# A recommendation tower on one core: GpSimd folds the gathered rows twice between its gathers

## The reference

```python
e = jnp.stack([tbl_0[ids[:, 0]], ..., tbl_31[ids[:, 31]]], axis=1)
z = jnp.sum(e, axis=-1)                                     # 32 sums
outer = jnp.einsum('bpd,pde,bpe->bp', e[:, II], kernels, e[:, JJ])   # 496 pairs
h = jnp.concatenate([z, outer, dense_ctx], axis=1)          # 544 values
h = jnp.maximum(h @ W_top1 + b_top1, 0.0)                   # 512
h = jnp.maximum(h @ W_top2 + b_top2, 0.0)                   # 256
y = h @ W_top3
```

## Time and profile before

| | before |
|---|---|
| median of 3 runs | 1091.63 us |
| profiled execution | 1090.3 us |
| its span | 1088.1 us |
| granted TensorE clock, mean | 0.914 |
| PE busy | 863.0 us, 79% |
| DVE busy | 636.6 us, 59% |
| ACT busy | 569.1 us, 52% |
| GpSimd (POOL) busy | 483.7 us, 44% |
| 512 gathers | 483.0 us, 943 ns each |
| DVE row sums, L371 | 64, 676 ns each |
| DVE products, L386 and L399 | 512, 1219 and 1218 ns each |

### The profile page before, as it was taken

How to read it: one execution, slowest core, us unless ns; L and a number is a source line. 1 busy time by engine, 2 the same in 40 slices (tenths; PEclk the granted TensorE clock), 3 DMA queues, 4 the chain that set the end, 5 groups by cost and what they waited for, 6 DMA issues and landing times.

```text
span 1088.1 us, 15106 instructions
## 1 busy us (share of the span) xinstructions
PE 863.0 (79%) x4112; PEld 294.6 (27%) x4112; DVE 636.6 (59%) x579; ACT 569.1 (52%) x4209; POOL 483.7 (44%) x518
## 2 busy tenths in 40 slices
PE   0312103989896999999879899998959899999998
PEld 0100001323232333332222233332312233333333
DVE  0110002977784766667766775676847656778960
ACT  0000000687775705686676526676747227687961
POOL 5777771003536554555545554455355545510000
PEclk9866555999997999999989999999979899999999
DMA  9211110000101110111101110011011101100000
GB/s 350 80 27 27 27 26 7 1 1 12 20 14 23 19 21 15 20 20 20 21 17 20 18 20 17 19 20 21 14 21 19 20 17 20 19 7 2 2 1 0
DMA packets 19803, 28.39 MB, mean 26 GB/s; under 512 B 8900, under 2 KB 9412, under 8 KB 18824
## 3 DMA queue, kind: packets, MB, share of 16 engines
q0 software_dynamic: 16384, 16.81, 8.4%
q1 hardware_dynamic: 3336, 10.63, 2.6%
HBM read 27.40 MB, written 0.01 MB: 25 GB/s over the span
## 4 chain that ended last, share of the span: by engine, by line
PE 63%; another core or an unknown queue 17%; issue 6%; DVE 6%; ACT 3%; DMA 2%; POOL 1%; SPq 1%; DVEq 0%; POOLq 0%
PE m_ps L498 27%; PE acc L526 14%; PE m_ps L513 9%; DVE prod L386 4%; PE tr L426 2%; ACT turned L323 2%; PE tr L446 2%; PE tr L456 2%; PE tr L450 2%; DMA w_sb<-in_w 2%; DVE turned L399 2%; POOL gathered L237 1%; PE tr L443 1%; PE m_ps L500 1%
## 5 line engine op out<-in xcount | busy, mean ns | idle before, releaser
L237 POOL DMA_INDIRECT gathered<-in_tbl,idx x512 | 483.0, 943 | 476.0 <-DVE prod L386 128.3
L386 DVE TENSOR_TENSOR prod<-m_ps,x_t 128x1024 f32<-128x1024 f32 x384 | 459.2, 1219 | 314.2 <-remote 169.5
L323 ACT ACTIVATE turned<-turned 128x64 f32<-128x64 f32 x2048 | 490.5, 241 | 105.1 <-DVE turned L399 86.5
L498 PE MATMUL m_ps<-x_t,k_sb 64*128 64x512 f32 x768 | 413.1, 641 | 138.2 <-DVE prod L386 67.7
L500 PE MATMUL m_ps<-x_t,k_sb 64*128 64x512 f32 x768 | 414.0, 642 | 0.0
L323 ACT ACTIVATION_READ_ACCUMULATOR turned<-turned 128x1 f32 x2048 | 384.5, 188 | 13.5 <-issue 13.3
L498 PEld LDWEIGHTS m_ps<-x_t,k_sb 64*128 64x128 f32 x768 | 130.8, 192 | 365.7 <-issue 272.2
L526 PE MATMUL acc<-prod,sel 128*32 128x512 f32 x1536 | 196.3, 631 | 0.0
L399 DVE TENSOR_TENSOR turned<-m_ps,gathered 128x1024 f32<-128x1024 f32 x128 | 155.9, 1218 | 60.1 <-PE m_ps L513 22.5
L274 ACT ACTIVATE x_t<-tr 128x512 f32<-128x512 f32 x64 | 37.6, 587 | 244.8 <-remote 155.0
L513 PE MATMUL m_ps<-k_sb,x_t 64*128 64x512 f32 x512 | 138.7, 618 | 6.7 <-DVE turned L399 6.7
(11 more groups left out here) (36 smaller groups left out, 113.4 us busy)
## 6 DMA issues: line engine op xcount, KB each, us to landing
gathered<-in_tbl,idx POOLq DMA_INDIRECT x512
k_sb<-in_kmat SPq DMA_DIRECT2D x7, 1024.0 KB, 11.3
w_sb<-in_w SPq DMA_DIRECT2D x1, 1280.0 KB
k_sb<-in_kmat SPq DMA_DIRECT2D x2, 256.0 KB, 3.3
k_sb<-in_kmat SPq DMA_DIRECT2D x1, 512.0 KB, 5.4
w_sb<-in_w SPq DMA_DIRECT2D x1, 512.0 KB
idx<-in_ids SPq DMA_DIRECT2D x1, 256.0 KB, 2.7
z_sb<-in_dense_t SPq DMA_DIRECT2D x4, 32.0 KB
```

The lines of the kernel that those rows point to most:

```text
L237: nc.gpsimd.indirect_dma_start(out=gathered[:, t, G % GR, f * D:(f + 1) * D], out_offset=None, in_=tables[2 * (STAGES - 1 - a) + f], in_of ...
L323: last = nc.scalar.activation(row, row, ACT.Copy, accum_out=z_turned[:, t, 16 * c + n:16 * c + n + 1])
L386: nc.vector.tensor_tensor(prod[:, r % PR, :, :], m_ps[:, p % MR, :, :], other, ALU.mult).then_inc(prod_ready, 1)
L498: nc.tensor.matmul(m_ps[:, p % MR, 0, :], k_sb[0:D, at, :], x_t[0:D, (q * STAGES + a0) % XR, :], start=True, stop=True)
```

## The change

Between its gathers GpSimd now also adds: when gather k - 4 has landed, `halve` adds the two halves of its 64 values into `x_half` (32 values, two places), and `fold` adds the two halves of that into `x_fold` (16 values, a ring of FR = 8 stages), one gather later. DVE's `sum_x` sums the 16 values of each row from `x_fold` and waits for the folds, not for the gathers. The ring of gathered stages is freed for the sums by the halving. Stages of later batches are transposed, copied and summed from step 97 on, 8.5 steps apart, and at the latest 4 steps in front of their first use, which for a = 0 to 15 is 97, 105, 114, 122, 131, 133, 136, 139, 146, 153, 163, 173, 186, 200, 216, 224; their gathers are asked for at the same steps as before. In batch 0, stages 14 and 15 stand at steps 86 and 90. The row sums are transposed at step 116, before at 80. `x_t` has room for 18 stages, before 20, and `y` is written into a row of `h2_sb`.

```diff
-XR = 20
+FR = 8
+XR = 18
...
-    return NS * (q - 1) + 82 + 8 * a
+    return NS * (q - 1) + min(97 + 17 * a // 2, NS + STEP_OF["even", FIRST[a]] - 4)
+
+
+def step_of_gather(q, a):
+
+    return NS * (q - 1) + 58 + 8 * a
...
-    AHEAD.setdefault((0, max(0, min(_s, 81 - 2 * (STAGES - 1 - _a))) if _a > 1 else 0), []).append(("x", 0, _a))
+    AHEAD.setdefault((0, max(0, min(_s, 90 - 4 * (STAGES - 1 - _a))) if _a > 1 else 0), []).append(("x", 0, _a))
...
-    AHEAD.setdefault((_q, 80), []).append(("s", _q, 0))
+    AHEAD.setdefault((_q, 116), []).append(("s", _q, 0))
...
+            def halve(k):
+                G, n = divmod(k, GATHERS)
+                t, f = divmod(n, 2)
+                at = gathered[:, t, G % GR, f * D:(f + 1) * D]
+                pool.wait_ge(gather_landed[k % IN_FLIGHT], (k // IN_FLIGHT + 1) * 16)
+                if k > 1:
+                    pool.wait_ge(x_folded, k - 1)
+                nc.gpsimd.tensor_tensor(x_half[:, k % 2, :], at[:, 0:D // 2], at[:, D // 2:D], ALU.add).then_inc(x_halved, 1)
+
+            def fold(k):
+                G, n = divmod(k, GATHERS)
+                t, f = divmod(n, 2)
+                pool.wait_ge(x_halved, k + 1)
+                if n == 0 and G >= FR:
+                    pool.wait_ge(x_summed, G - FR + 1)
+                nc.gpsimd.tensor_tensor(x_fold[:, G % FR, t, f, :], x_half[:, k % 2, 0:D // 4],
+                                        x_half[:, k % 2, D // 4:D // 2], ALU.add).then_inc(x_folded, 1)
...
+                if k >= IN_FLIGHT:
+                    halve(k - IN_FLIGHT)
+                if k > IN_FLIGHT:
+                    fold(k - IN_FLIGHT - 1)
+                if n == 0 and G >= GR:
+                    old_q, old_a = divmod(G - GR, STAGES)
+                    pool.wait_ge(tr_filled, place("x", old_q, old_a))
+                    pool.wait_ge(x_halved, (G - GR + 1) * GATHERS)
+                    if old_a // COLS:
+                        pool.wait_ge(prod_ready, old_q * NS + LAST_TURNED[old_a // COLS] + 1)
+                if q:
+                    pool.wait_ge(prod_ready, step_of_gather(q, a) + n)
+                col = ((q * STAGES + a) * 2 + f) * TILES + t
+                nc.gpsimd.indirect_dma_start(
...
 def keep_h2(q, n):
     act.wait_ge(tr_filled, place("h2", q, n))
+    if q and n == 0:
+        act.wait_ge(y_stored, 16 * q)
...
-                for landed in gather_landed:
-                    dve.wait_ge(landed, (G + 1) * GATHERS // IN_FLIGHT * 16)
+                dve.wait_ge(x_folded, (G + 1) * GATHERS)
...
-                                        gathered[:, :, G % GR, :].rearrange("p t (f d) -> p t f d", d=D),
+                                        x_fold[:, G % FR, :, :, :],
```

More of the change, by code:

```diff
@@ L160, in dlrm_tower @@
         z_sb = sb("z_sb", [P, NZ, QB])
+        x_half = sb("x_half", [P, 2, D // 2])
+        x_fold = sb("x_fold", [P, FR, TILES, 2, D // 4])
         z_nat = sb("z_nat", [P, 2, TILES, SUM_ROWS])
@@ L165, in dlrm_tower @@
         h2_sb = sb("h2_sb", [P, H2 // P, QB])
-        y_sb = sb("y_sb", [1, QB])
+        y_sb = h2_sb[0:1, 0, :]
         idx = sb("idx", [P, NQ * F * TILES], i32)
@@ L191, in dlrm_tower @@
         reduced = sem("reduced")
+        x_halved = sem("x_halved")
+        x_folded = sem("x_folded")
         x_summed = sem("x_summed")
@@ L217, in _ @@
             pool.wait_ge(idx_loaded, 16)
-            for G in range(NQ * STAGES):
-                q, a = divmod(G, STAGES)
[L220 to L240, removed]
@@ new lines, in _ @@
+            for k in range(NQ * STAGES * GATHERS):
+                G, n = divmod(k, GATHERS)
+                q, a = divmod(G, STAGES)
+                t, f = divmod(n, 2)
+                if k >= IN_FLIGHT:
[12 more added lines that the diff above has]
+                nc.gpsimd.indirect_dma_start(
+                    out=gathered[:, t, G % GR, f * D:(f + 1) * D], out_offset=None, in_=tables[2 * (STAGES - 1 - a) + f],
+                    in_offset=bass.IndirectOffsetOnAxis(ap=idx[:, col:col + 1], axis=0),
+                ).then_inc(gather_landed[k % IN_FLIGHT], 16)
@@ L242, in _ @@
+            for k in range(NQ * STAGES * GATHERS - IN_FLIGHT, NQ * STAGES * GATHERS):
+                halve(k)
+                fold(k - 1)
+            fold(NQ * STAGES * GATHERS - 1)
         @block.sync
@@ L260, in _ @@
                     sp.wait_ge(tr_kept, place("y", q - 1, 0))
-                    sp.dma_start(out[:, (q - 1) * QB:q * QB], y_sb[:]).then_inc(y_stored, 16)
+                    sp.dma_start(out[:, (q - 1) * QB:q * QB], y_sb).then_inc(y_stored, 16)
             sp.wait_ge(y_ready, 1)
-            sp.dma_start(out[:, LAST * QB:NQ * QB], y_sb[:]).then_inc(y_stored, 16)
+            sp.dma_start(out[:, LAST * QB:NQ * QB], y_sb).then_inc(y_stored, 16)
             sp.wait_ge(y_stored, 16 * NQ)
@@ L285, in keep_y @@
                 act.wait_ge(tr_filled, place("y", q, 0))
-                if q:
-                    act.wait_ge(y_stored, 16 * q)
-                nc.scalar.activation(y_sb[:], tr[0:1, :], ACT.Copy).then_inc(tr_kept, 1)
+                nc.scalar.activation(y_sb, tr[0:1, :], ACT.Copy).then_inc(tr_kept, 1)
             def keep_sums(q):
@@ L349, in _ @@
                                      bias=b1_sb[:, n:n + 1]).then_inc(h1_ready, 1)
+            act.wait_ge(y_stored, 16 * LAST)
             for n in range(H2 // P):
@@ L354, in _ @@
             act.wait_ge(y_summed, 1)
-            act.wait_ge(y_stored, 16 * LAST)
-            nc.scalar.activation(y_sb[:], tr[0:1, :], ACT.Copy).then_inc(y_ready, 1)
+            nc.scalar.activation(y_sb, tr[0:1, :], ACT.Copy).then_inc(y_ready, 1)
         @block.vector
```

## The result

The changed kernel takes 958.79 us (median of 4 runs, 958.0 to 959.47) where the kernel before took 1090.12 (4 runs, 1086.85 to 1092.18): a ratio of 0.8797, 95% interval 0.8771 to 0.8824. The forecast was 970, with a range of 930 to 1125. The profiled execution took 958.0 us, its span is 956.2. The size came out close; part of that closeness is errors that cancel, and the condition behind the gain turned out to be narrower than the prediction has it. "The standstill" is the state that the prediction describes: gathers go on, and the other engines hardly compute.

What follows compares the result with a forecast made beforehand. Gathers leaving GpSimd every 1.25 us were taken to bound the kernel by nearly stopping other engines. Spaced at 1.70, GpSimd's path gives 962 and PE's 946; 962 plus 8 for mutual waits gives 970 us, range 930 to 1125.

Steps and rivals of the forecast that it cites:

- The cause: Gathers back to back at 1.25 us nearly stop other engines; 130 us at the start and 39 a batch open.
- The period: GpSimd's gather spacing with both adds: 1.25 + 0.45 = 1.70 us, each add 0.13 plus about 0.1 issue.
- My term for GpSimd: GpSimd's whole path: 3.7 + 512 x 1.70 + 3 = 877, then landing, last steps, tail and outside: 962 us.
- PE's chain: Batch 0's first layer at 297 us from stage 9, three batches at 203, tail 38, outside 2.2: 946 us.
- the list of signs: Expected in the trace after: gathers 1.6 to 1.8 us apart, batch 0's first layer near 320, batches 200 to 220.
- 196 + 7: PE's time for a later batch: 196 us, and some for gathers at 5 in 8 us, making 203.
- Later transposes and the ring of 18 at nothing: Later batches' transposes from step 97, and the smaller x_t ring: same PE, ACT and DVE instruction numbers, cost 0.
- 8 more: Added because GpSimd's and PE's paths, 16 us apart, wait for each other in turn at gates: 8 us.
- Dear adds: Rival at GpSimd's adds: each further 0.1 us of period costs 51 us, no gain at 1.95; chance 0.12.
- Standstill from GpSimd busy without pause: Rival: adds between gathers cure nothing, the start lasts 52 us longer, 1142 us; chance of standstill kept 0.11.
- Only DVE's sums: Rival: only DVE's lighter sum gains, at most 26 us, 1064 to 1090; shares 0.24 with two other cases.
- Half a cure: Rival: start cured, 39 us a batch stay through bursts behind gates, 1048 us; shares 0.24 with two other cases.

Runs made afterwards that it cites:

- order alone: The changed kernel without GpSimd's adds, DVE summing all 64 gathered values: 1127.9 us, ratio 1.0174 to the kernel before.
- MEMSET of 1: The kernel before with a one-column MEMSET on GpSimd in front of each gather: 1091.94 us, ratio 0.9998.
- halves alone: The changed kernel with only the first add, DVE summing 32 values from a ring of 6: 1088.22 us, ratio 0.9818 to the kernel before.
- MEMSET of 384: The kernel before with a 384-column MEMSET on GpSimd in front of each gather: 937.72 us, ratio 0.8596.
- Group C: Third set of runs, on chip 12: longer MEMSETs, two gathers under way, half rows, each against the kernel before, which took 901.95 us there.
- adds alone: The kernel before with both GpSimd adds between gathers, results unused, old order, ring and sums: 942.07 us, ratio 0.8498.
- full-sum kernel: The changed kernel, adds kept but folds unread, DVE summing the 64 gathered values: 958.12 us, ratio 0.864 to the kernel before.
- adds in batch 0 alone: The kernel before with both adds, results unused, for batch 0's gathers only: 1041.41 us, ratio 0.9546.
- half-row kernel: The kernel before, each gather fetching 32 of 64 values a row, DVE clearing the tile first: 902.86 us, ratio 1.0024.
- group A: First set of runs, on chip 4, testing parts of the change against the kernel before, which took 1108.31 us there.
- group B: Second set of runs, on chip 12, mainly testing spacing without adds against the kernel before, which took 1091.29 us there.

## Why the prediction was right, and where it was not

**The cause.** The step was to read 17% of unknown queue and 169.5 us of "remote" as the effect of gathers 1.25 us apart. Wherever the standstill stood, the runs bear it out: 1.25 (order alone, and for most gathers the MEMSET of 1) and 1.40 (halves alone) have it, 1.55 (MEMSET of 384) and 1.57 (adds) don't. What the prediction missed is that it took this for a property of the kernel. Group C has the same spacing without the effect. "The rows show the condition, the spacing" was too strong: they showed one condition of at least two.

**The period.** Predicted 1.70, measured 1.57. The adds themselves are dearer than my 0.13 us each, 0.26 and 0.22; I took their length as lying between one element and 128, and the fixed part weighs more than that. But the 0.1 of issue for each was not there: an add starts 0.02 us behind a gather, and a gather 0.16 us behind an add, where it was 0.30 behind another gather. My term for GpSimd goes by 512 x 0.13 = 67 us, from 962 to 895, and no longer bounds the whole. Its last gather starts at 826.92 where the working had 877 at 1.70, and has 810 at 1.57; the rest is waiting at the gates. Batch 0's 128th starts at 206.97, where I had 222.

**PE's chain.** First layer of batch 0 predicted near 320 (297 + 14 x 1.45 = 317), measured 318.2. That is luck. At the measured period stage 9 lands 80 x 0.13 = 10 us sooner and is folded 1 us sooner behind it, so my working gives 306. What fills the other 12 us is GpSimd. It issues gathers 1.57 us apart without a pause from batch 0's last into batch 1's, and PE has to wait for two of them:

```profile
297.49 1.09 PE L457 MATMUL tr<-ident,gathered 128*128 128x128 f32 x4 [4.40 <-DMA gathered<-in_tbl,idx]
309.96 1.09 PE L457 MATMUL tr<-ident,gathered 128*128 128x128 f32 x4 [7.63 <-DMA gathered<-in_tbl,idx]
```

The chain runs on GpSimd from 236.8 us to the gather of 307.36, as it did from 48 to 138 us. I took one of two chains to bound from start to end; in the run GpSimd bounds most of the way to 308 us, and PE from there. Batches predicted at 203, within 200 to 220 in the list of signs: 210.5. From the last first layer to the end, 216.9. In the order of before and without a standstill a batch takes 203.5 (adds alone: 320.21, 523.73, 727.26), so 196 + 7 was well sized, and what is missing is the next point.

**Later transposes and the ring of 18 at nothing.** This is the term that was mis-sized: 16 to 20 us, not 0. I counted the same instructions and the room of the ring, and didn't ask what a transpose stands behind. The chain of the kernel after has two pieces of ACT in batches 1 and 2, here those of batch 2 (batch 3 has only the short one); then PE around the second:

```profile
587.69 2.42 ACT turned L355 x21
...
659.11 10.06 ACT turned L355 x85
```
```profile
667.07 0.66 PE L457 MATMUL tr<-ident,gathered 128*128 128x128 f32 x4
...
671.19 0.63 PE L457 MATMUL tr<-ident,gathered 128*128 128x128 f32 x4 [2.40 <-ACT x_t L306]
```

ACT copies each transposed stage out of the one tr tile, and the same queue holds the sums of the turned products, 16 pairs of instructions and 3.8 us (32 x 10.06 / 85) for each. Where two uses of tr come close together among turned steps, the second waits for the copy of the first, and that copy for the sums. The piece of 10.06 us is 42 pairs, more than two products' worth; the copy behind it ends at 671, and PE, whose transpose of 667 filled tr, stands 2.40 us. At 592 it is 2.31, in front of a layer's matmuls into tr. The adds-alone kernel has no ACT piece over 1.6 us in the same batch. These two idles are 4.7 of the 7.0 us that a batch lost; where the other 2.3 lie I did not trace. (That the order costs and the ring does not was read from this chain, not tried by itself.)

**How 970 came near 959.** 970 was GpSimd's 962 and 8 more. With the measured period GpSimd's chain gives 895 and PE's 946 - 11 = 935. The way from 935 to 958: 12 us for the first layer of batch 0, 15 for two batches at 210.5 instead of 203, less 4 for the last stretch (216.9, where the working has 203 - 20 + 38 = 221). The 16 us of the order are in these differences: against adds alone 7 in each of two batches and 4 in the last stretch, less 2 at the start. So the standstill was priced right; the period, too long by 0.13, stood in for the order and for GpSimd's part of the start, and the nearness of 970 is in part luck.

**DVE.** Sum predicted 0.27 us, measured 277 ns; worth nothing, as booked (958.12 without it; 958.79 with it, in another group). Predicted "remote" in front of the products under 20 us: 0.

**The rivals.** Dear adds: the period stayed far from 1.95. Standstill from GpSimd busy without pause: refuted, it is busy 102 of 115 us with PE at work. Only DVE's sums: refuted by the full-sum kernel. Half a cure did not come for the change, but it is what adds in batch 0 alone show (1041, where I had 1048 for a cured start with 39 us a batch left; its start is cured only for 53 of 84 us and it bears no cost of the order, so the two numbers meet partly by chance). GpSimd over 90% of its stretch was wrong: 713.1 of some 828 us is 86%.

## What to carry to other kernels

When the chain names an unknown queue and an engine waits on "remote" for work that is long done, look at what else issues in that stretch, and space it with something worthless before building something useful: a long MEMSET per gather, beside a short one, settled here what the change could only suggest. A step that is moved "with the same instructions" still has to be placed in the queue of every engine it uses; price it by what stands in front of it there. And time the old kernel in several sessions: its time moved by 17% between two of them, more than the change was worth, and a speedup against one condition can be a loss against the other.

## What was not expected of the hardware

- The kernel before has two levels, about 1090 to 1108 us in three groups of runs and 902 in a fourth, within 1% inside each. Two of these groups ran on one chip. The half-row kernel at the lower level has gathers as long and as far apart as the kernel before at the higher one; the kernel before was not traced at the lower.
- Under the standstill's condition, with four gathers under way and even spacing, 1.40 us (group A) still has it and 1.55 (group B) and 1.57 (group A) don't.
- Under it GpSimd's own short MEMSETs wait on "remote" too, up to 1.18 us.
- Short GpSimd operations are nearly all fixed cost: adds of 32 and 16 columns took 262 and 225 ns, a MEMSET 0.11 us for 1 column, 0.28 for 203, 0.36 for 297 and 0.43 for 384. Between gathers two adds lengthen the period by 0.32 us only.
- Under the standstill other engines slow within a run of their own instructions too. ACT in the kernel before, whose sums run without idle time elsewhere:

```profile
330.51 0.20 ACT L323 ACTIVATION_READ_ACCUMULATOR turned<-turned 128x1 f32 x1 [0.23 <-issue]
331.23 0.26 ACT L323 ACTIVATE turned<-turned 128x64 f32<-128x64 f32 x1 [0.51 <-issue]
...
332.65 0.20 ACT L323 ACTIVATION_READ_ACCUMULATOR turned<-turned 128x1 f32 x1 [0.92 <-issue]
```

It waits 0.2 to 0.9 us for nothing but its next instruction. This suggests that it is the supply or release of instructions that the gathers hold up, and not data; no run here tested it.
